# A four-layer gated attention kernel on one core: four changes to the order of work at the seams of the layers and groups

## The reference

```python
x = x + tanh(g_xattn[0]) * L0_xattn(layernorm(x), ctx, ...)     # 32 heads of 128, 8 key heads, biases
x = x + tanh(g_ffn[0])   * L0_ffn(layernorm(x), ...)            # ternary weights, norm, tanh, rounding
x = x + tanh(g_xattn[1]) * L1_xattn(layernorm(x), ctx, ctx, ...) # 32 heads, rotary embedding, causal
x = x + tanh(g_ffn[1])   * L1_ffn(layernorm(x), ...)            # 4-bit weights with low-rank terms
x = x + tanh(g_xattn[2]) * L2_xattn(layernorm(x), ctx, ...)     # 16 heads of 96, keys from ctx and x
x = x + tanh(g_ffn[2])   * L2_ffn(layernorm(x), ...)            # routed low-rank experts
x = x + tanh(g_xattn[3]) * L3_xattn(layernorm(x), ctx, mask, ...) # 32 heads, RMS norm of q and k
x = x + tanh(g_ffn[3])   * L3_ffn(layernorm(x), ...)
return x
```

## Time and profile before

| what | value |
|---|---|
| median of three runs | 2061.44 us |
| the profiled execution | 2061.95 us |
| its span | 2060.1 us |
| granted TensorE clock, mean over the span | 0.970 |
| PE busy | 1916.9 us, 93% |
| DVE busy | 1401.2 us, 68% |
| ACT busy | 1062.1 us, 52% |
| POOL busy | 930.5 us, 45% |
| first attention layer's loop, 20 to 505 us | PE busy 480.8 of 485 |
| second attention layer, 600 to 942 us | PE busy 319.1 of 342, DVE 279.6 |
| third attention layer, 1054 to 1412 us | PE busy 326.0 of 358 |
| fourth attention layer, 1463 to 2010 us | PE busy 532.0 of 547 |

### The profile page before, as it was taken

How to read it: one execution, slowest core, us unless ns; L and a number is a source line. 1 busy time by engine, 2 the same in 40 slices (tenths; PEclk the granted TensorE clock), 3 DMA queues, 4 the chain that set the end, 5 groups by cost and what they waited for, 6 DMA issues and landing times.

```text
span 2060.1 us, 33785 instructions
## 1 busy us (share of the span) xinstructions
PE 1916.9 (93%) x11138; PEld 1643.2 (80%) x11138; DVE 1401.2 (68%) x2507; ACT 1062.1 (52%) x2413; POOL 930.5 (45%) x998
## 2 busy tenths in 40 slices
PE   6999999999769999998999999987899999999998
PEld 5788888888557888886767888876688889888986
DVE  6777777777678888886235555547476676667675
ACT  4776767667344545442125544533265555556552
POOL 3664655545546666653313222323254444445432
PEclk9999999999989999999989999998899999999998
DMA  4222222212211121211210010001110111011101
GB/s 146 88 67 75 76 74 91 72 47 68 92 46 57 52 66 51 76 52 36 66 56 14 27 34 6 21 1 58 57 47 17 47 47 47 17 47 47 37 1 48
DMA packets 47775, 106.79 MB, mean 52 GB/s; under 512 B 6129, under 2 KB 19953, under 8 KB 44193
## 3 DMA queue, kind: packets, MB, share of 16 engines
q1 hardware_dynamic: 47648, 105.14, 15.8%
HBM read 98.37 MB, written 6.75 MB: 51 GB/s over the span
## 4 chain that ended last, share of the span: by engine, by line
PE 79%; DVE 11%; issue 5%; ACT 4%; POOL 1%; DMA 0%; DVEq 0%; SPq 0%; ACTq 0%; POOLq 0%
PE psX L423 27%; PE psO L423 13%; PE psQ L423 12%; PE psS L423 11%; PE psT L878 7%; PE psSX L423 3%; PE psT L423 2%; PE psX L957 1%; ACT p_sb L1292 1%; DVE nbias L1050 1%; DVE p_sb L1047 1%; DVE pT_lo L1072 1%; DVE ln_stat L551 1%; DVE p_sb L1056 1%; DVE xn_f L561 1%
## 5 line engine op out<-in xcount | busy, mean ns | idle before, releaser
L1450 POOL TENSOR_SCALAR p_sb<-p_sb,rrec 128x512 f32<-128x512 f32 (+1 forms) x288 | 233.6, 811 | 501.9 <-DVE rrec L1068 501.9
L1303 ACT ACTIVATE pT_hi<-psT 128x512 fp32r<-128x512 f32 (+2 forms) x384 | 234.9, 612 | 314.2 <-PE psT L878 313.3
L1072 DVE TENSOR_TENSOR pT_lo<-psT,pT_hi 128x512 fp32r<-128x512 f32 (+2 forms) x384 | 271.2, 706 | 71.7 <-ACT pT_hi L1303 71.0
L423 PE MATMUL psO<-pT_hi,v_hi 128*128 128x256 f32 (+1 forms) x832 | 255.4, 307 | 22.4 <-DVE pT_lo L1072 16.4
L423 PE MATMUL psO<-pT_lo,v_hi 128*128 128x256 f32 (+1 forms) x832 | 237.2, 285 | 0.0
L423 PE MATMUL psO<-pT_hi,v_lo 128*128 128x256 f32 (+1 forms) x832 | 237.0, 285 | 0.0
L878 PE MATMUL psT<-ident,p_sb 128*128 128x128 f32 x1408 | 213.0, 274 | 10.6 <-POOL p_sb L1450 7.2
L878 PEld LDWEIGHTS psT<-ident,p_sb 128*128 128x128 f32 x1408 | 172.4, 140 | 49.4 <-POOL p_sb L1450 9.8
L423 PE MATMUL psQ<-xnT_hi,wq_hi 128*128 128x512 f32 x428 | 178.1, 416 | 10.8 <-DVE qscr L1032 8.0
L423 PEld LDWEIGHTS psO<-pT_hi,v_hi 128*128 128x128 f32 (+1 forms) x832 | 155.2, 187 | 29.9 <-DVE pT_lo L1072 24.9
L720 POOL TENSOR_TENSOR wq_lo<-wq_f,wq_hi 128x512 fp32r<-128x512 f32 x108 | 139.6, 1293 | 78.4 <-ACT wq_hi L705 78.4
(11 more groups left out here) (486 smaller groups left out, 5177.2 us busy)
## 6 DMA issues: line engine op xcount, KB each, us to landing
wq_f<-in_a_wq SPq DMA_DIRECT2D x108, 256.0 KB, 2.7
wo_f<-in_a_wo SPq DMA_DIRECT2D x24, 1024.0 KB, 4.9
wkv_f<-in_a_wkv SPq DMA_DIRECT2D x16, 512.0 KB, 3.7
mask_sb<-in_codes SPq DMA_DIRECT2D x32, 174.0 KB, 2.4
qscr<-in_amax SPq DMA_DIRECT2D x32, 174.0 KB, 2.3
w<-qscr SPq DMA_DIRECT2D x32, 174.0 KB, 1.8
wo_f<-in_f_wT SPq DMA_DIRECT2D x3, 1024.0 KB, 5.0
wo_f<-in_a_wo SPq DMA_DIRECT2D x4, 768.0 KB, 4.3
```

The costliest lines, as they stand in the source:

```text
L423: mm = pe.matmul(dst, w, m, start=(first and k == 0), stop=(last and k == n - 1))
L1072: L.t_lo.inc(dve.tensor_tensor(pT_view(L, pT_lo, j), t_view(L, j), pT_view(L, pT_hi, j).bitcast(F32), ALU.subtract))
L1303: L.t_hi.inc(act.activation(pT_view(L, pT_hi, j), t_view(L, j), ACT.Copy))
L1450: L.s_norm.inc(pool.tensor_scalar(p_view(L, j), p_view(L, j), rrec[:, j:j + 1], 1.0, ALU.mult, ALU.mult))
```

## The change

- First to second layer: SP issues the second layer's first weights right behind the feed-forward weights (`second_sync`), key and value weights first; ACT copies wkv 0, wkv 1, wq 0, wq 1 in this order; POOL makes only the two wkv low parts ahead of its powers, and the two wq parts behind the feed-forward bias. DVE does `o_low` ahead of the threshold.
- Second layer: the query product of slot (3,1), with DVE's `q_front` and POOL's `q_sum`, goes to slot (3,0).
- Third layer: DVE adds output tile 1 in slot (0,3) ahead of `pT_low` (PE already made it ahead of the transposes).
- Fourth layer: `k1` goes from slot (3,2) to slot (3,3), and there ahead of the query product on PE, ACT and DVE.

```diff
-    dict(kind="rope", ..., settle=2, q_slot=(0, 0, 1, 1),
+    dict(kind="rope", ..., settle=2, q_slot=(0, 0, 1, 0),
...
-         prep={(1, 3): ["n0"], (2, 2): ["n1"], (2, 3): ["n2"], (3, 0): ["k0"], (3, 1): ["n3"], (3, 2): ["k1"]}),
+         prep={(1, 3): ["n0"], (2, 2): ["n1"], (2, 3): ["n2"], (3, 0): ["k0"], (3, 1): ["n3"], (3, 3): ["k1"]}),
...
+    def ahead_of_query(self, h, j):
+        return self.rms and (h, j) == (3, 3)
...
+        FIRST_KV, FIRST_Q = (("wkv", 0), ("wkv", 1)), (("wq", 0), ("wq", 1))
...
+        def second_sync(sp):
+            L, names = layers[1], a["attn1"]
+            layers[0].wq_lo.wait(sp, 4 * layers[0].n)
+            layers[0].wkv_lo.wait(sp, layers[0].n)
+            layers[0].wv_lo.wait(sp, layers[0].n)
+            L.wkv_dma.inc(sp.dma_start(wkv_f[:, :, :], names["wkv"][0, :, :, :]), 16)
+            for h in (0, 1):
+                L.wq_dma[h].inc(sp.dma_start(wq_f[:, h, :], names["wq"][h, :, :]), 16)
...
-            first()
+            if L.i != 1:
+                first()
...
# PE, DVE and ACT, head(g, h), ahead of the query's step
+                    if L.ahead_of_query(h, j):
+                        while units:
+                            use(g, units.pop(0), g.to(1))
...
# DVE, head(g, h)
+                    units = L.slot_uses(g, h, j)
+                    if L.packed and len(units) == 2 and units[0][0] == "out":
+                        use(g, units.pop(0), g.to(-1))
                     pT_low(g, h, j)
...
# DVE, tail(g)
+                o_low(g, 3)
                 if L.i == 0:
                     f0_threshold(dve)
-                o_low(g, 3)
...
# ACT, tail(g)
-                    first_high(act, layers[1])
+                    for kind, piece in FIRST_KV + FIRST_Q:
+                        w_high(act, layers[1], kind, Group(0), piece)
...
# POOL, tail(g)
-                    first_low(pool, layers[1])
+                    for kind, piece in FIRST_KV:
+                        w_low(pool, layers[1], kind, Group(0), piece)
...
# SP, f0_sync
             sp.dma_start(wo_f[:, :, :], a["f0_wT"]).then_inc(f0_wdma, 16)
+            second_sync(sp)
...
# POOL, between ln_gpsimd(1) and the feed-forward block, behind f0_bias_low
+                    for kind, piece in FIRST_Q:
+                        w_low(pool, layers[1], kind, Group(0), piece)
```

More of the change, by code:

```diff
@@ L70 @@
                {(2, 2): ["k0"], (2, 3): ["k1"], (3, 2): ["n0"], (3, 3): ["n1"]})),
-    dict(kind="rope", hd=128, groups=8, keys=256, slots=2, nbuf=2, ahead=2, settle=2, q_slot=(0, 0, 1, 1),
+    dict(kind="rope", hd=128, groups=8, keys=256, slots=2, nbuf=2, ahead=2, settle=2, q_slot=(0, 0, 1, 0),
          outs=OUT_PAIRS, splits=SPLIT_PAIRS,
@@ L771, in first @@
             def first():
[L772 to L776, removed]
+                if L.i == 2:
                     sp.wait_ge(f1_lo, H1C)
@@ L1249, in head @@
                         dq_vector(dve, g, h, "low" if j == 1 else "high")
+                    if L.ahead_of_query(h, j):
+                        while units:
+                            use(g, units.pop(0), g.to(1))
                     if j == L.q_slot(g, h) and L.query(g, h, L.q_lead):
                         (q_front if L.rope else q_low)(*L.query(g, h, L.q_lead))
-                    for u in L.slot_uses(g, h, j):
+                    for u in units:
                         if u[0] == "v":
@@ L1259, in tail @@
             def tail(g):
+                o_low(g, 3)
                 if L.i == 0:
                     f0_threshold(dve)
-                o_low(g, 3)
-                if L.i == 2:
+                elif L.i == 2:
                     f2_router(dve)
```

## The result

The kernel after the change takes 2051.21 us (median of six runs, 2048.94 to 2055.27), against 2062.18 us for six runs of the kernel before (2059.55 to 2064.55). The ratio is 0.9947, with an interval of [0.9934, 0.996]: 11 us or 0.5% faster. The profiled execution took 2048.94 us.

A forecast was written before the change was run, and what follows sets the result against it. PE, busy 93% of the span, was taken as the bound, so only its waits and clock could be won. 2061.95 - 5.4 - 10.4 + 8.9 - 0.5 = 2054.55 us profiled, less 0.51: 2054.0 us; range 2044 to 2059.

The forecast's parts named there:

- First layer's end: First to second layer: DVE's 5.19 us wait for POOL's power goes, the first add comes 0.40 sooner; -5.4 us.
- Rival 4: First layer's end gives only 1 to 2 us, DMAs sharing the queue: 2057.5 to 2058.4 us; chance 0.07.
- Third layer: DVE's earlier add saves PE 2.44 us three times, 7.3 us, plus 3.1 us of clock; -10.4 us.
- The clock's part: Third layer: half clock behind two of three removed waits goes, 1.57 and 1.54 us, together 3.1 us.
- My upper end of 12: Third layer: 12 us if the two half-clock stretches behind the fourth long wait go as well.
- Second layer: PE's three waits become one of about 2.8 us: +1.1 us, plus 7.8 us of half clock; +8.9 us.
- 5 of 7 by my share: Second layer: half clock behind the long wait in 5 of 7 groups, 1.55 us each, 7.8 us.
- Rival 1: Second layer: clock holds, two drops at most; 3.1 instead of 7.8 us, 2049.4, with none 2046.3; chance 0.17.
- rival 2: Second layer: every group pays for the clock; 10.9 instead of 7.8 us, 2057.1 us; chance 0.13.
- rival 5: Second layer: half clock lasts two stretches behind each of 7 waits; 21.7 instead of 7.8 us, 2067.9; chance 0.05.
- Fourth layer: PE's 0.77 us wait for scaled keys moves to the scores; -0.07 us a group, 7 groups; -0.5 us.
- The sum: Whole kernel: the four parts lead from 2061.95 to 2054.55 us profiled, less 0.51: 2054.0 us.

The follow-up runs named there:

- e1: Kernel before with only the parts at the end of the first layer; 2055.10 us, ratio 0.9962.
- e7: Change without its second-layer part, and in slot (3,3) ACT's key copy ahead of the exponential, DVE's low part ahead of `pT_low`; 2039.07 us, ratio 0.9891.
- e10: The whole change, unchanged, profiled in another execution; 2055.13 us.
- e3: Kernel before with only the third layer's part; 2051.95 us, ratio 0.9955.
- e5: Kernel before with the second layer's query product in (3,0) on PE alone, DVE's rotation and POOL's sum staying in (3,1); 2071.69 us, ratio 1.0029.
- e8: Whole change, with the second layer's query product in slot (0,0) ahead of the values half that waits for `pT_low`; 2071.54 us, ratio 1.0041.
- e2: Kernel before with only the second layer's part; 2074.07 us, ratio 1.006.
- e11: The change without its third and fourth layers' parts; 2064.99 us.
- e12: Kernel before with only the second layer's part, profiled in another execution; 2072.29 us.
- e9: Change with earlier fourth-layer key copies, query product ahead of the values half in (0,0), POOL's wq low part ahead of the query's sum; 2040.05 us, ratio 0.9891.

## Why the prediction was right, and where it was off

The kernel came out at 2051.21 us, inside the range and 2.8 us under the forecast of 2054.0, and faster, as forecast. (The kernel before came out 0.7 us above the 2061.44 that I started from, so the forecast gain was 7.4 us and the measured one 11.0.) The mechanisms held in three parts, and the fourth came out with the wrong sign. By its steps:

- **First layer's end, -5.4 predicted, -5.9 in the trace after**, 5.3 in e1, and 4.6 to 5.9 in the eight profiled executions that hold this part, 5.2 in the mean. The mechanism is as described: the normalisation starts at 536.20 without a wait (536.7 forecast), and the next limit is again the output tile, 0.18 us. Rival 4 is out: no execution gained as little as its 1 to 2 us. Inside the sum the landing of the weights (1 us too late) and POOL's low parts (3.97 for my 2.51) were both off, with opposite sign. POOL's first low part now overlaps DVE's ternary weights (530.42 to 532.69) where before it stood alone, and the trace tells the two low parts apart: the first took 2.72 us and the second, behind the overlap, 1.29 like those before. e1 (2.68 and 1.29) and e7 (2.66 and 1.29) show it again. In e10, where DVE's instruction came later, POOL's took 2.16 and 3.32 us and DVE's 3.24 instead of 2.27. So it is the overlap that costs; what the two engines share there no run here tells.
- **Third layer, -10.4 predicted, -11.9 measured.** 3 x 2.44 of waits is exact (2.63 to 0.19). The clock's part was 3.1 by my sum and is 4.6, because the two half-clock stretches behind the fourth long wait shrank too: 0.50 and 0.50 before, 0.73 in the same first stretch after. My upper end of 12 had named exactly that case, and e3 shows it with the part alone (12.0 us). Every profiled execution with this part gains 11.8 to 12.0 us here; those without it lie between -1.7 and +1.6 us of the execution before, from the clock alone. So 11.9 is the gain over one execution of the kernel before, certain to about 1.6 us.
- **Second layer, +8.9 predicted, +6.6 in the trace after.** The wait has moved as worked out: one wait of 2.76 us (2.8), `pT_low` last, 0.19 us a group (0.16), seven times. The mis-sized term is the number of groups that pay for the clock: 5 of 7 by my share, 3 in this execution, at 1.57 us (1.55). The five executions put it at 4.2 of 7 and the loop at 9.4 us. So the term was sound as a mean, and near it by luck, since the share of three in four came from four waits; the profiled execution was a cheap one, and with 5 stretches it would have taken some 3 us more. The timed runs of the change spread over 6.3 us, and those of e5 over 12.8, which fits a count that changes from run to run. Rival 1 (two drops at most) missed that one profile by a stretch; what rival 2 says of every group came true in the profiled executions of e5 and e8, and what rival 5 says of a double price for single groups of e2 and e11 (3.0 us more than 44.7), but not throughout.
- **Fourth layer, -0.5 predicted, +0.7 measured.** That the wait would only be moved was right, and so was its size (0.71, I had 0.6 for it). But the price is 0.1 us a group more and not 0.07 less. The step that failed is the last one, from the wait to the group. Set 12.75 us later, by the row maxima ahead of that slot, the times after are those that I worked out: the low part ends at 1617.52 (1617.55) and PE starts the scores at 1617.65 (1617.6). The sum took the low part's end for PE's start, and that alone made it -0.07 against 1617.62. And it put at nothing what follows a wait: the second matmul of the scores starts 0.34 us after the first (1605.24 - 1604.90), where in the kernel before it started 0.22 after it (1617.84 - 1617.62). I had counted such a refill of 0.1 us in the second layer, and not here. Together that is near 0.15 us for this group, and the row maxima have 0.7 for the seven. The first time in the chain is also mis-added (1613.90 + 1.49 is 1615.39, not 1615.35), which the trace happens to forgive: 1602.60 there is 1615.35.
- **The sum**: 2061.95 - 5.9 - 11.9 + 6.6 + 0.7 = 2051.5, and what no part explains (-1.6, -0.8 and -0.1) leads to 2049.0, the profiled time within 0.1. The profiled execution is 5.6 us under its forecast of 2054.55. The parts make 3.1 of that: the second layer 2.3, the third 1.5 and the first 0.5 less than forecast, the fourth 1.2 more. The other 2.5 belong to no part. The median is only 2.8 us under its forecast, since the profiled execution was the fastest of the six; that the median came so close is in part luck, as a part of the gain that I had not forecast belongs to none of the four parts.

The Trainium skill, TensorE: Matmul & The Clock Gate, section on HAM oscillation, describes a kernel that paid anew at every single wait of its loop, waits of some 3 to 5 us for a DMA. Here, with waits of 1.9 to 2.9 us, that happened in the profiled executions of e5 and e8 (seven of seven each), and not in the five that hold the wait for `pT_low`: 21 of 35. For those five, a price at every wait bounds the cost from above, and the mean was 0.6 of it.

## What to carry to other kernels

Ask of a wait that you remove where PE's idle time goes. If the stretch is another engine's, drawing PE's work forward only gathers PE's idle time into one wait, and this kernel shows three waits of together 2.08 us costing no clock in 49 groups where one of 2.75 us cost 1.6 us in 21 of 35. To move a product forward, first move forward what the next engine does with its result: the same edit of the fourth layer cost 0 to 4 us with ACT's copy behind the exponential, and gave 4.1 us in the median and 5.6 in that layer's part of the trace with ACT's and DVE's copies first. And where the clock's share is in the sum, one profile is one draw: look at it in a second execution before you put a number on it.

## What I had not expected of the hardware

The same loop, with the same wait of 2.75 us at the same place, ran the work behind it at 1.2 GHz in one execution and at 2.4 GHz in the next: 3 and 5 of seven times in the change, 5 and 3 in e2 and e12, 5 in e11. The Trainium skill, TensorE: Matmul & The Clock Gate, section "What's actually happening", says of a kernel's start that the count of slow matmuls differs from run to run of one kernel; these traces show the same in the middle of a kernel whose PE is 93% busy. Nor had I expected a wait as short as e5's 1.9 us, with 0.4 us close in front of it, to be followed by half clock seven times of seven in the execution profiled, while e9's 1.1 us never was. And a stretch could be followed by another: the groups of 47.7 us in e2 and e11 have one twice as long.
